# Two more couples of layer 3 masked by VectorE, turning back in two tasks, new orders of work

## The reference, cut to what matters

```python
x = _layernorm(x + _L0_gnn_ref(x, adj, W, a))    # attention, relu
x = _layernorm(x + _L1_gnn_ref(x, adj, adj, W, a))    # 8 heads, attention, elu
x = _layernorm(x + _L2_gnn_ref(x, adj, rel_weights, ...))    # mean of neighbours, product
x = _layernorm(x + _L3_gnn_ref(x, adj, W))    # 4 heads of dot-product attention
```

```python
Wh = jnp.einsum('bsf,hfd->bhsd', features, W)    # 4 heads of width 32
scores = jnp.einsum('bhsd,bhtd->bhst', Wh, Wh) / jnp.sqrt(jnp.float32(D))
scores = jnp.where(adj_matrix[:, None, :, :] > 0, scores, NEG_INF)
attn = jax.nn.softmax(scores, axis=-1)
h = jnp.einsum('bhst,bhtd->bhsd', attn, Wh)
```

## Time and profile before

| what | value |
|---|---|
| median of 3 runs | 2420.53 us (2417.59 to 2421.4) |
| profiled execution | 2423.86 us, its span 2422.1 us |
| TensorE busy | 2242.2 us, 93% |
| VectorE busy | 1977.9 us, 82% |
| ScalarE busy | 1938.1 us, 80% |
| POOL busy | 192.2 us, 8% |

### The profile page before, as it was taken

One profiled execution on the slowest core, in us unless ns is written; L12 is line 12 of the kernel. 1 busy time (PEld: TensorE's weight loads), 2 busy tenths in 40 slices (PEclk: granted clock), 3 DMA queues, 4 the chain that ended last, 5 costly groups with the idle time before them and its releaser, 6 DMA issues.

```text
span 2422.1 us, 56777 instructions
## 1 busy us (share of the span) xinstructions
PE 2242.2 (93%) x23701; PEld 1528.8 (63%) x23701; DVE 1977.9 (82%) x4206; ACT 1938.1 (80%) x2166; POOL 192.2 (8%) x134
## 2 busy tenths in 40 slices
PE   6667999999999999999999999999999999999977
PEld 5567566585765748576575857658585665857442
DVE  4587788988888898888889888888888889888767
ACT  3858798797988879788787979879797987979735
POOL 0000000001000100100010000001000010010000
PEclk8888999999999999999999999999999999999998
DMA  5625016043251613416062251605225160411100
GB/s 92 159 59 125 19 63 140 28 107 70 70 132 54 141 36 97 80 63 140 29 148 54 69 108 63 140 28 130 63 63 123 61 142 28 106 36 65 34 19 18
DMA packets 190864, 193.76 MB, mean 80 GB/s; under 512 B 129368, under 2 KB 165328, under 8 KB 187728
## 3 DMA queue, kind: packets, MB, share of 16 engines
q1 hardware_dynamic: 183008, 132.99, 20.4%
q0 software_dynamic: 7600, 57.15, 12.1%
HBM read 151.26 MB, written 40.43 MB: 79 GB/s over the span
## 4 chain that ended last, share of the span: by engine, by line
PE 64%; ACT 13%; DVE 11%; issue 7%; DMA 5%; SPq 0%; POOL 0%; ACTq 0%; POOLq 0%; DVEq 0%
PE kp L1148 13%; PE kp L1131 10%; PE fp L1022 9%; PE kp L1003 6%; PE fp L947 6%; ACT ramp L1330 5%; ACT weight L1378 4%; PE kp L1072 4%; PE kp L1124 4%; DVE weight L1580 3%; DMA shared<-shared 2%; PE kp L1069 2%; DVE weight L1820 2%; PE fp L871 2%; PE kp L1165 1%
## 5 line engine op out<-in xcount | busy, mean ns | idle before, releaser
L1330 ACT ACTIVATE ramp<-s1row,tbig 128x1024 fp8e4<-128x1024 f32 x854 | 910.9, 1156 | 12.1 <-DMA s1row<-s_rows_dram 11.9
L1378 ACT ACTIVATE weight<-kp,shift 128x1024 f32<-128x1024 f32 x480 | 511.0, 1112 | 272.1 <-PE kp L1131 266.3
L1148 PE MATMUL kp<-weight,w 128*33 128x512 f32 x1920 | 447.4, 597 | 2.3 <-DVE weight L1820 1.3
L1022 PE MATMUL fp<-vh_parts,weight 128*128 128x102 bf16 x8192 | 418.1, 209 | 30.8 <-issue 11.2
L1022 PEld LDWEIGHTS fp<-vh_parts,weight 128*128 128x128 fp8e4 x8192 | 392.9, 98 | 79.9 <-issue 54.1
L1674 DVE TENSOR_TENSOR weight<-ramp,AT 128x512 int32<-128x512 int32 x512 | 341.7, 687 | 116.3 <-ACT ramp L1330 106.6
L1820 DVE SCALAR_TENSOR_TENSOR weight<-AT,weight 128x1024 f32<-128x1024 fp8e4 x272 | 319.8, 1219 | 46.9 <-ACT weight L1378 46.9
L1131 PE MATMUL kp<-shared 32*128 32x512 f32 x1920 | 274.1, 640 | 23.3 <-ACT weight L1378 23.2
L1148 PEld LDWEIGHTS kp<-weight,w 128*33 128x33 f32 x1920 | 96.7, 110 | 280.2 <-issue 247.9
L947 PEld LDWEIGHTS fp<-features,weight 128*128 128x128 f32 x1840 | 208.8, 192 | 41.1 <-issue 24.4
L1003 PE MATMUL kp<-vh_parts,AT 128*128 128x136 bf16 x3072 | 231.6, 239 | 0.0
(11 more groups left out here) (251 smaller groups left out, 2729.8 us busy)
## 6 DMA issues: line engine op xcount, KB each, us to landing
s1row<-s_rows_dram SPq DMA_DIRECT2D x128, 512.0 KB, 4.7
adj_bf_dram<-in_adj_dram POOLq DMA_DIRECT2D x15, 2048.0 KB, 15.2
AT<-turned POOLq DMA_DIRECT2D x15, 1024.0 KB, 9.6
x<-in_x_dram SPq DMA_DIRECT2D x16, 512.0 KB, 6.7
out_dram<-elu SPq DMA_DIRECT2D x16, 512.0 KB, 10.4
xfT<-s_row_dram SPq DMA_DIRECT2D x15, 512.0 KB, 4.5
shared<-shared SPq DMA_DIRECT2D x30, 256.0 KB, 3.7
elu<-x POOLq DMA_DIRECT2D x15, 512.0 KB, 4.6
```

The source lines that it names most:

```text
L1022: last = pe.matmul(fp[:, 1 + t // 4, col:col + 2 * PARTS * C1], edges[:, u % B_RING, t * P:(t + 1) * P], vh_parts[:, jt, h, :, :, :].rearr ...
L1148: last = pe.matmul(kp[side(h), 0, :], values3(b)[:, (2 * J + x) * H3 + h, :], weight3[:, w % P_RING, x * HALF:(x + 1) * HALF], start=(J == ...
L1330: act.activation(ramp[:, u % R_RING, :], s1row[:, h % S_RING, :] if b or h else kp_pair, ACT.Relu, bias=tbig1[:, jt, h:h + 1], scale=BIG, ...
L1378: act.activation(weight3[:, w % P_RING, :], score_banks(b, w).rearrange("p a n -> p (a n)"), ACT.Exp, bias=shifts3(b)[:, h:h + 1], scale=R ...
```

## The change

`MASKED` names ten couples where it named eight. `layer3_turn_back` becomes two tasks, one per half; the second waits for the first by semaphore as before, but other tasks may stand between. And the orders on all engines are different, for the sections at both ends too; the total of steps is 138 where it was 135.

```diff
-    MASKED = (4, 6, 8, 10, 11, 12, 13, 14)
+    MASKED = (3, 5, 6, 8, 9, 10, 11, 12, 13, 14)
...
-            def layer3_turn_back(b, k):
-
-                pe.wait_ge(sum3_ready.sem, sum3_ready.of(b))
-                if k is not None and k < NB - 1:
-                    pe.wait_ge(sum2_read.sem, sum2_read.of(k))
-                for x in range(2):
-                    if x:
-                        pe.wait_ge(first_turned.sem, first_turned.of(b))
...
+            def layer3_turn_back(b, k, x):
+
+                if x:
+                    pe.wait_ge(first_turned.sem, first_turned.of(b))
+                else:
+                    pe.wait_ge(sum3_ready.sem, sum3_ready.of(b))
+                    if k is not None and k < NB - 1:
+                        pe.wait_ge(sum2_read.sem, sum2_read.of(k))
...
-                if m is not None and s == at["turn_back"]:
-                    layer3_turn_back(m, k)
+                for x in range(2):
+                    if m is not None and s == at["turn_back"][x]:
+                        layer3_turn_back(m, k, x)
```

Of the tables, the lines for a full section that the steps of the prediction touch (TensorE, VectorE, POOL, SP):

```diff
-                 52, 56, 61, 65, 70, 75, 82, 84, 86, 89, 92, 96, 100, 102, 104], self2=0, shift3=45, sources1=93,
-                 spread0=53, spread1=97, sum1=[20, 21, 23, 26, 29, 30, 31, 32], sum2=[1, 2, 3, 4, 8, 10, 15, 16],
-                 top0=48, turn0=[22, 24], turn1=88, turn2=98, turn3=37, turn_back=28, unit0=[72, 73, 74, 76, 77, 79,
-                 80, 81], unit1=[5, 6, 7, 9, 11, 12, 13, 14, 17, 18, 19, 25, 27, 33, 35, 38, 41, 42, 44, 46, 49, 50,
+                 55, 58, 62, 67, 73, 75, 82, 84, 86, 88, 91, 96, 101, 103, 105], self2=0, shift3=47, sources1=94,
+                 spread0=49, spread1=98, sum1=[19, 21, 24, 25, 28, 29, 33, 35], sum2=[1, 2, 3, 4, 9, 11, 14, 16],
+                 top0=45, turn0=[26, 30], turn1=90, turn2=99, turn3=38, turn_back=[22, 27], unit0=[72, 74, 76, 77, 78,
+                 79, 80, 81], unit1=[5, 6, 7, 8, 10, 12, 13, 15, 17, 18, 20, 23, 31, 32, 36, 39, 41, 43, 44, 48, 51,
...
-                 finish1=65, finish3=25, head1=[8, 12, 20, 33, 40, 48, 53, 61], lengths3=34, low2=91, masked3=[-1, -1,
-                 -1, -1, 60, -1, 68, -1, 74, -1, 77, 81, 83, 86, 88, -1], maxima1=80, maxima3=36, maximum0=51,
-                 most0=44, norm0=75, norm1=79, norm3=26, out2=15, ramps=[-1, -1, -1, -1, 1, -1, -1, -1, 7, -1, -1, -1,
-                 -1, -1, -1, -1, -1, -1, -1, -1, -1, 31, -1, -1, 41, -1, -1, 43, -1, -1, -1, -1], relu2=23, rest2=90,
-                 shift0=52, shift3=38, shifts1=82, stats2=17, stats3=50, tail3=57, top0=39, top1=78, unit0=[62, 63,
-                 64, 66, 67, 69, 70, 71], unit1=[0, 2, 3, 4, 5, 6, 9, 10, 11, 13, 14, 16, 18, 19, 22, 24, 27, 28, 29,
-                 30, 32, 35, 37, 42, 45, 46, 47, 49, 54, 56, 58, 59], z0=55),),
+                 finish1=65, finish3=25, head1=[6, 13, 20, 31, 42, 47, 54, 61], lengths3=34, low2=93, masked3=[-1, -1,
+                 -1, 56, -1, 67, 70, -1, 75, 78, 79, 83, 85, 89, 90, -1], maxima1=82, maxima3=37, maximum0=41,
+                 most0=39, norm0=76, norm1=81, norm3=26, out2=15, ramps=[-1, -1, -1, -1, 1, -1, -1, -1, 7, -1, -1, -1,
+                 -1, -1, -1, -1, -1, -1, -1, -1, -1, 33, -1, -1, 44, -1, -1, 49, -1, -1, -1, -1], relu2=23, rest2=91,
+                 shift0=53, shift3=40, shifts1=84, stats2=17, stats3=46, tail3=58, top0=35, top1=80, unit0=[62, 63,
+                 64, 66, 68, 69, 71, 72], unit1=[0, 2, 3, 4, 5, 8, 9, 10, 11, 12, 14, 16, 18, 19, 21, 24, 27, 28, 29,
+                 30, 32, 36, 38, 43, 45, 48, 51, 52, 55, 57, 59, 60], z0=50),),
...
-            (dict(adjacency=3, narrow=0, residual3=-1, rstd0=4, rstd1=5, rstd2=1, rstd3=2, rstd_tail=-1),),
-            (dict(adjacency=5, narrow=3, residual3=2, rstd0=6, rstd1=7, rstd2=0, rstd3=1, rstd_tail=4),),
+            (dict(adjacency=4, narrow=1, residual3=-1, rstd0=3, rstd1=5, rstd2=0, rstd3=2, rstd_tail=-1),),
+            (dict(adjacency=6, narrow=4, residual3=2, rstd0=5, rstd1=7, rstd2=0, rstd3=1, rstd_tail=3),),
...
-            (dict(adjacency=1, far=6, out=-1, sources=[2, 3, 5, 4, 8], sources_ahead=[13, 12, 11], spread_row=9,
-                 store_row=7, store_sources=10, x=0),),
-            (dict(adjacency=7, far=6, out=10, sources=[1, 0, 3, 5, 4], sources_ahead=[13, 12, 14], spread_row=9,
+            (dict(adjacency=0, far=5, out=-1, sources=[2, 3, 4, 7, 6], sources_ahead=[13, 12, 11], spread_row=9,
+                 store_row=8, store_sources=10, x=1),),
+            (dict(adjacency=4, far=7, out=10, sources=[0, 1, 3, 5, 6], sources_ahead=[13, 12, 14], spread_row=9,
```

More of the change, by code:

```diff
@@ L1151, in layer3_values @@
                 last.then_inc(weight3_used.sem, 1)
-            def layer3_turn_back(b, k):
-                pe.wait_ge(sum3_ready.sem, sum3_ready.of(b))
-                if k is not None and k < NB - 1:
-                    pe.wait_ge(sum2_read.sem, sum2_read.of(k))
-                for x in range(2):
-                    if x:
-                        pe.wait_ge(first_turned.sem, first_turned.of(b))
-                    for g in range(len(GROUPS)):
-                        for n, t in enumerate(GROUPS[g]):
-                            for h in range(x, H3, 2):
-                                col = (n * H3 + h) * C3
-                                last = pe.transpose(kp[:, g, col:col + C3],
-                                                    o3T[side(h), h // 2, t * P:(t + 1) * P],
-                                                    ident[side(h), side(h)])
-                    last.then_inc((sum3_turned if x else first_turned).sem, 1)
+            def layer3_turn_back(b, k, x):
[5 more added lines that the diff above has]
+                        pe.wait_ge(sum2_read.sem, sum2_read.of(k))
+                for g in range(len(GROUPS)):
+                    for n, t in enumerate(GROUPS[g]):
+                        for h in range(x, H3, 2):
+                            col = (n * H3 + h) * C3
+                            last = pe.transpose(kp[:, g, col:col + C3],
+                                                o3T[side(h), h // 2, t * P:(t + 1) * P],
+                                                ident[side(h), side(h)])
+                last.then_inc((sum3_turned if x else first_turned).sem, 1)
             pe.wait_ge(consts_made, 3)
```

204 lines of the change are left out of this document (102 added, 102 removed).

## The result

The change made the kernel slower: 2435.09 us (median of 4 runs, 2433.15 to 2436.36) against 2420.13 (2417.59 to 2421.4), a ratio of 1.0062 with a 95% interval of 1.0045 to 1.008. Forecast were 2382.7 and a range of 2361 to 2410.

The account below looks back on a forecast made before the run. TensorE, busy 138.5 of 143.4 us, was taken to pace each section. -28.8 + 18.3 - 2.5 - 15.8 - 9.0 = -37.8 us, from the median of 2420.53 to 2382.7 us; range 2361 to 2410.

Parts of the forecast that it names:

- the price of the added multiplications: VectorE's four new multiplications per batch: one of them, 1.22 us a section, taken as exposed, +18.3 us in all.
- Other swaps of order: Remaining reorderings on the engines: not priced apart, bounds of 5 us gain or loss per section, taken as nothing.
- the dense stretch: Stretch behind couple 3's new mask: VectorE busy 22.55 of 23.0 us, two masked couples before (4, 6), two after (5, 6).
- Products, -28.8: TensorE's products with the constant, dropped for two couples of 15 batches at 0.96 us each: -28.8 us.
- The fourth rival: No change: TensorE's freed time turns into waits for ScalarE's exponentials; 2418.0 us, chance 0.06.
- Turning back and the clock, -2.5 and -15.8: TensorE's split turning back: hidden wait between halves -2.5 us; clock holding in 11 of 13 sections -15.8 us.
- The first full section, -9.0: First full section: source rows no longer queue behind the adjacency matrix load, -9.0 us (0 to -9.0).
- The hand-over: Projections' DMA hand-over before the first scores, queued behind SP's transposing load: taken as covered; uncovered up to 8 us a section.
- The ends: Sections at both ends: their new orders got no price of their own, beyond other swaps taken as nothing.
- The fifth rival: Slower: VectorE becomes the bound between couples 3 and 14, every new multiplication on the path; 2462 us, chance 0.11.
- the turning point: Share of multiplications exposed at which the kernel turns slower: 43% with clock and load unchanged, 77% with both gains.
- the spare 21 us a section: VectorE's idle time per full section, busy 121.8 of 143.4 us, read as room for the added multiplications.

Follow-up runs that it names:

- a_no9: The changed kernel with couple 9 masked by TensorE's products again, nine couples on VectorE: 2441.73 us, 1.006 of the kernel before.
- a_no3: The changed kernel with couple 3 masked by products again, other orders kept: 2449.1 us, 1.0096 of the kernel before.
- c0: Base: the kernel before (eight couples, old orders) with the turning back split and the first full section's adjacency load moved later: 2405.46 us, 0.9916.
- c0_m39: c0 with couples 3 and 9 masked by VectorE too, ten couples without the change's new orders: 2428.28 us, 1.0026 of the kernel before.
- c0_m9: c0 with couple 9 masked by VectorE in the last stretch, nothing else moved: 2431.09 us, 1.003 of the kernel before.
- c0_dense: c0 with the change's dense-stretch order on TensorE, VectorE and ScalarE, couple 5 masked in place of 4: 2458.58 us, 1.0143 of the kernel before.
- c0_noact: c0_dense with ScalarE kept in its old order: 2465.39 us, 1.0161 of the kernel before.
- c0_act: c0 with only ScalarE's dense stretch in the change's order: 2424.55 us, 1.0001 of the kernel before.
- c0_m5: c0 with couple 5 masked by VectorE as well, nine couples, three of them in the dense stretch: 2465.07 us, 1.018 of the kernel before.
- a_no5: The changed kernel with couple 5 masked by products again, every other order kept: 2445.95 us, 1.0084 of the kernel before.
- c0_v5: c0 with one TensorE task moved, couple 5's values to behind the scores of couple 7: 2411.09 us, 0.9955 of the kernel before.
- a_no89: The changed kernel with couples 8 and 9 masked by products again: 2448.66 us, 1.0096 of the kernel before.
- a_joined: The changed kernel with the turning back's second half right behind the first in the full sections: 2443.43 us, 1.0071 of the kernel before.
- a_no5v: a_no5 with couple 5's values moved back into the dense stretch, behind layer 0's fifth edge task: 2463.62 us, 1.016 of the kernel before.
- a_dense: The changed kernel with the old dense-stretch order on all three engines, couple 4 masked in place of 5: 2454.12 us, 1.0123 of the kernel before.
- a_4for5: The changed kernel with couple 4 masked in place of 5, couple 5's values back in front of layer 0's edge work: 2461.97 us, 1.0147.
- c0_m3: c0 with couple 3 masked by VectorE between edge tasks 28 and 29, its values behind couple 4's scores: 2416.17 us, 0.9958 of the kernel before.
- c0_split_start: The run of c0 itself, with the split turning back and the later first-section adjacency load alone: 2405.46 us, 0.9916 of the kernel before.

## Why the prediction was wrong

**The step that failed** is the price of the added multiplications, +18.3 us or 1.22 a section, with the sentence behind the orders, "Other swaps of order I cannot price apart; [...] I take nothing". The runs give four corners of a full section, the third by adding +0.3 (a_no9) and +0.8 (a_no3) to the kernel after, which takes for granted that the two add up:

```
                         8 couples on VectorE    10 couples
orders of before (c0)         142.7                144.1
orders of the change          146.0 (added up)     144.9
```

On the old orders two more couples make the section 1.4 us longer, where the forecast's terms (1.22 less 1.92 of products) make it 0.7 shorter. If the products are worth their 1.92 there, four multiplications cost 144.1 - 142.7 + 1.92 = 3.3 us a section, 50 us in 15 sections instead of 18.3, and eat the 28.8 of the products. The net price is shown by c0_m39, and nearly all of it comes with couple 9 (c0_m9), whose mask stands behind the statistics of layer 1's output.

The new orders make each masked couple a gain (0.3 to 0.8 a section), but lie some 3.3 us higher to begin with, and with ten couples they take 0.8 more than the old ones. c0_dense (+3.7, of them 0.8 a wait of its own) shows that the orders of the dense stretch, taken together, cost most of this, and c0_noact (+4.0) that ScalarE's isn't needed for it; c0_act shows that ScalarE's order alone can cost 1.2. By the three parts the loss lies in layer 0's sums (+1.1) and, the greater part, behind them (+2.1 to 2.3). What is not shown is which move does it. I had put it down to the second masked couple inside VectorE's pass, which got 2.3 us longer. For it: in c0_m5 a second couple inside, with TensorE's and ScalarE's old orders, costs 2.1 to 2.3 us where the clock holds. Against it: a_no5 takes that couple out of the change's pass, and the section grows; c0_act has a pass as long with one couple inside, and costs 1.2. A rival that fits the parts stays open: the values of couple 5, 1.84 us that TensorE could do while it waited for VectorE, wait for their mask and stand behind the dense stretch in the change. Moved there alone, without the mask, they cost 0.2 (c0_v5), as layer 0's sums got 0.9 shorter and the part behind them 1.1 longer; with VectorE pacing the sums, that shortening could fail to come.

The prediction read VectorE 22.55 of 23.0 us busy in the dense stretch, and wrote "two masked couples before (4, 6) and two after (5, 6)". The count was right, and the places were left out: in the tables `masked3` 4 is step 60 and the edge tasks begin at 62, while `masked3` 5 is step 67, between 66 and 68.

**Products, -28.8.** 360 of line 1124 and 332 multiplications of line 1821 came as said, and TensorE is busy 1.8 us less. What a couple's products are worth was wrong for the last stretch: 0.35 for couples 8 and 9 (a_no89), since the round of 3.50 us takes the rest; 0.8 for couples 3 and 5. The fourth rival had this mechanism, waits for ScalarE's exponentials, and I gave it 0.06; it forecast no change, since it left the other gains out.

**Turning back and the clock, -2.5 and -15.8.** Right in kind: no fall in 13 sections, and 7 of 13 when the halves are joined. In the base c0 half of it stayed, 0.8 of 1.6 us a section; what came next was a wait of 0.91 us for VectorE's x, which I had not named. The page TensorE: Matmul & The Clock Gate of the Trainium skill, section HAM oscillation, ties falls to idle gaps. The falls of before and of a_joined don't agree, as TensorE idles nowhere ahead of them (3.40 of 3.40 us busy in the window of the fall too). Those of a_no5v, a_dense and c0_m5 do: they come with waits of 2.36, 2.35 and 3.08 us.

**The first full section, -9.0.** Right: -11.1 in the change, -12.7 in the base, where the split is in it too; TensorE's 9 us wait is gone. **The hand-over**, for which I took nothing: TensorE waited 15.8 us in all for that DMA before the products of line 1124, 1.2 in the median full section, and in the kernel after it waits for it in none of the 13. Little came of it, as other waits took its place: with couple 3 on products, as in the base, the part ahead of layer 0's sums is 84.2 us (a_no3) against 84.4. **The ends**, where I took nothing: batch 15's section -3.5, the last +4.4, +0.9 together; their orders weren't tried by themselves.

**The fifth rival**, slower by VectorE between couples 3 and 14 (chance 0.11), came true in its sign. It set the turning point at 77% of the multiplications exposed if the other gains hold. By the sum of a section, 143.5 - 1.4 - 0.2 - 1.9 = 140.0 with all of them hidden and 144.9 measured, the 4.9 us would be the price of all four, 4.88 us. That they agree is a coincidence: with every multiplication on the path, a section would get 1.5 us shorter (2.44 less 0.96) for each couple taken back, and it got longer in a_no9, a_no5, a_no3 and a_no89. It deserved more all the same: the spare 21 us a section were a mean, and I let them outweigh the two stretches where VectorE was full.

## What to carry to other kernels

A mean share of 85% says nothing on where new work goes. Where engines pass work round over few buffers, the same number of tasks in a stretch is not the same order: look at what stands between the first and the last task of such a round on each engine, before and after, and at what filler leaves it. And price work taken off the pacing engine by the next round that closes there (here scores, exponentials, scores, 3.50 us against 3.87 for a couple with its products), not by its own length.

When an experiment moves one task, look at which tasks it brings side by side. Three of these runs made a wait of 2.4 us of their own in that way, and say little on what they were made for.

Take the parts of a change that stand alone: the split and one moved load, without masks or searched orders, ran at 2405.46 us, 0.9916 of the kernel before.

## What the runs showed of the hardware

- TensorE's clock fell to its lower level (0.50) for 3.4 us behind 32 transposes of 33 columns with TensorE busy all the time, in 11 of 13 sections before and 7 of 13 in a_joined; with 16 and 16 apart it stayed at 2.4 GHz in all 13. Such a fall cost 1.1 to 1.4 us.
- It also fell with single waits of TensorE of 2.35 us (a_dense), 2.36 (a_no5v) and 3.08 (c0_m5), in 12, 10 and 11 of 13 sections; in c0_m5 such a fall cost 1.6 to 1.9 us. In a_4for5 waits of 2.2 and 2.4 us in each of 13 sections brought but 2 falls, both in the same one. So the length of the wait alone doesn't settle it; what else does stays open.
- A hand-over by DMA that TensorE waited some 1.3 us for in most sections of c0_m3 took longer in one of 13, 2.81 us, and the clock fell behind that too. In c0_split_start it fell in one section in which that wait was 1.39 us, and that section was 1.8 us longer than the median. The row of c0_m3:

```profile
1245.53 1.02 PE L1169 MATMUL kp<-AT,big 128*128 128x512 fp8e4 x4 [2.81 <-DMA shared<-shared]
```
